# Asking for each stream transfer two steps after its piece instead of three

## The reference, cut to what matters

```python
xz = jnp.einsum('bld,ed->ble', hidden_states, in_proj_w)
x, z = jnp.split(xz, 2, axis=-1)
xc = silu(causal_conv(x))                        # 4 taps
x_dbl = jnp.einsum('bld,ed->ble', xc, x_proj_w)  # -> dt_r, Bc, Cc
delta = softplus(dt_r @ dt_proj_w.T + dt_proj_bias)
def step(h, inp):                                # over time, per channel and state n (16 of them)
    dA = jnp.exp(delta_t[..., None] * A)
    h = h * dA + (delta_t * x_t)[..., None] * B_t[:, None, :]
    y_t = jnp.einsum('bdn,bn->bd', h, C_t)
y = (y + xc * D_param) * silu(z)
x = x + y @ out_proj_w.T
x = x + moe(x @ W.T + adapter(x))                # 16 experts, top 4, and a shared expert
```

## Time and profile before

| | |
|---|---|
| median of 3 runs | 1827.28 us (1825.8 to 1832.31) |
| the profiled execution | 1825.8 us, its span 1824.0 us |
| mean granted TensorE clock | 0.961 of full speed |
| PE busy | 1656.9 us (91%) |
| DVE busy | 1418.4 us (78%) |
| POOL busy | 1090.5 us (60%) |
| ACT busy | 843.1 us (46%) |
| transfers of B rows (`b_all`) | 128, 256 KB each, 3.2 us from issue to landing (median) |
| transfers of weight tiles (`wt`) | 116, 256 KB each, 3.1 to 3.9 us (medians by source) |

### The profile page before, as it was taken

One profiled execution on the slowest core, in us unless ns is written; L12 is line 12 of the kernel. 1 busy time (PEld: TensorE's weight loads), 2 busy tenths in 40 slices (PEclk: granted clock), 3 DMA queues, 4 the chain that ended last, 5 costly groups with the idle time before them and its releaser, 6 DMA issues. The chain is left out here.

```text
span 1824.0 us, 28764 instructions
## 1 busy us (share of the span) xinstructions
PE 1656.9 (91%) x8052; PEld 1217.0 (67%) x8052; DVE 1418.4 (78%) x1889; ACT 843.1 (46%) x1276; POOL 1090.5 (60%) x860
## 2 busy tenths in 40 slices
PE   8678877999998999989888999999999999999997
PEld 5255544665555655555455657788788999999997
DVE  3699999999999999999999726777355656565654
ACT  2666766667767676766664411000122323322331
POOL 0299689997799986999988470000144434343443
PEclk9878989999999999999999999999999999999999
DMA  5122212232232232222214352112157566566664
GB/s 131 36 64 64 72 45 69 65 92 82 81 110 76 87 93 79 95 92 66 87 59 127 104 167 68 70 69 96 42 127 183 132 175 158 142 134 171 138 170 71
DMA packets 130025, 181.96 MB, mean 100 GB/s; under 512 B 21443, under 2 KB 79555, under 8 KB 126788
## 3 DMA queue, kind: packets, MB, share of 16 engines
q1 hardware_dynamic: 109540, 131.85, 22.5%
q0 software_dynamic: 17888, 43.79, 12.4%
q10 hardware_dynamic: 2432, 4.33, 0.9%
HBM read 276.18 MB, written 37.36 MB: 172 GB/s over the span
## 5 line engine op out<-in xcount | busy, mean ns | idle before, releaser
L1244 POOL TENSOR_TENSOR arena_kept<-arena_kept,b_all 128x512 f32<-128x512 f32 x512 | 637.0, 1274 | 184.5 <-DVE arena_kept L1136 104.2
L1136 DVE TENSOR_TENSOR_SCAN arena_kept<-da,arena_kept 128x512 f32<-128x512 f32 x512 | 597.9, 1214 | 15.1 <-issue 8.7
L963 ACT ACTIVATE da<-arena_kept,a_neg 128x504 f32<-128x504 f32 x512 | 344.5, 685 | 183.1 <-DVE arena_kept L1136 175.8
L736 PE MATMUL hT<-ident_kept,arena_kept 128*128 128x128 f32 x2048 | 309.9, 296 | 122.4 <-DVE arena_kept L1136 61.5
L736 PEld LDWEIGHTS hT<-ident_kept,arena_kept 128*128 128x128 f32 x2048 | 252.6, 152 | 224.7 <-DVE arena_kept L1136 133.8
L1152 DVE SCALAR_TENSOR_TENSOR yacc<-hT,c_now,yacc 128x512 f32<-128x512 f32 x452 | 316.5, 744 | 7.7 <-PE hT L736 6.7
L2168 POOL DMA_INDIRECT out<-y,slots_kept x76 | 133.9, 1762 | 240.3 <-issue 177.9
L527 PE MATMUL bank<-hid,wt 128*128 128x512 f32 x512 | 237.7, 610 | 0.7 <-ACT hid L786 0.7
L527 PEld LDWEIGHTS bank<-hid,wt 128*128 128x128 f32 x512 | 97.0, 199 | 101.1 <-issue 100.2
L2038 ACT ACTIVATE gs<-egp 128x352 f32<-128x352 f32 x73 | 33.8, 463 | 237.4 <-PE eup L1348 236.8
L1800 POOL DMA_DIRECT2D slots_kept<-lists_kept x1 | 0.6, 567 | 211.9 <-DVE lists_kept L1752 211.9
(11 more groups left out here) (249 smaller groups left out, 3198.2 us busy)
## 6 DMA issues: line engine op xcount, KB each, us to landing
w_up_kept<-in_up_T SPq DMA_DIRECT2D x76, 1408.0 KB, 5.9
w_dn_kept<-in_dn_T SPq DMA_DIRECT2D x76, 768.0 KB, 7.2
b_all<-bt_scratch SPq DMA_DIRECT2D x128, 256.0 KB, 3.2
wt<-in_in_T SPq DMA_DIRECT2D x64, 256.0 KB, 3.2
wt<-in_out_T SPq DMA_DIRECT2D x32, 256.0 KB, 3.5
res<-in_x_pad SPq DMA_DIRECT2D x16, 256.0 KB, 4.2
x_scratch<-res SPq DMA_DIRECT2D x16, 256.0 KB, 2.1
wt<-in_w_T SPq DMA_DIRECT2D x16, 256.0 KB, 3.1
```

The source lines that it names most:

```text
L736: mm = nc.tensor.transpose(turned_in(j, m, t)[:, d * P:(d + 1) * P], h[:, m % RING, d, t * P:(t + 1) * P], ident[:])
L963: nc.scalar.activation(out[:, :, 1:], rows[:, :, 1:], ACT.Exp, scale=a_neg[:, d, n:n + 1]) \
L1136: nc.vector.tensor_tensor_scan(h[:, n % RING, i, :], da[i % RING][:], dbx[:, i, :], 0.0, ALU.mult, ALU.add).then_inc(scan_done, 1)
L1244: nc.gpsimd.tensor_tensor(dbx[:, i, :], u[:, d, :], b_all[:, m % RING, :], ALU.mult) \
```

## The change

The constant `LATER = 3` is gone, and 2 stands in its five places. A transfer that belongs to a piece of step `m` is now in SP's list behind the B row of step `m + 2`, where it was behind that of step `m + 3`. What each transfer waits for is the same, and so are the instructions of the other four engines. No transfer is added or taken away.

```diff
 SLOTS = 6
-LATER = 3
@@ tiles_due
-            at = of * STEPS + step_of(piece) + LATER
+            at = of * STEPS + step_of(piece) + 2
@@ SP's loop over the steps m of block j
                     for t in range(TB if j else 0):
-                        if m == step_of(f"xr{t}") + LATER:
+                        if m == step_of(f"xr{t}") + 2:
                             store_x1("body", j, t)
                     if j == NBLK - 1 and m == step_of(f"xr{TB - 1}") + 4:
                         load_res(NBLK)
-                    if j and m == step_of(f"w{KM - 1}") + LATER:
+                    if j and m == step_of(f"w{KM - 1}") + 2:
                         store_x2T("body", j)
                     for t in range(TB if j else 0):
-                        if m == step_of(f"row{t}") + LATER:
+                        if m == step_of(f"row{t}") + 2:
                             store_x2("body", j, t)
-            for m in range(STEPS, STEPS + LATER):
+            for m in (STEPS, STEPS + 1):
```

## The result

The changed kernel takes 1841.9 us (median of 9 runs, 1835.84 to 1847.78), the kernel before 1829.09 us in the same comparison: a ratio of 1.0078, with a 95% interval of 1.0057 to 1.0099. It is slower by 13 us by the medians and by 14 us by the ratio, and the interval lies clear of 1. The forecast was 1836 us, with "the same" a little ahead of "slower". The measured time lies 0.1 us under the upper end of the range, 1842; the likeliest case did not come, and the loss was 1.3 to 1.5 times the sum of 9.6 us.

What follows compares the result with a forecast made beforehand. DVE, 97% busy in block 1, was taken to set the pace. Late B rows at steps 5, 9 and 12 cost 3.2 us in each of blocks 1 to 3, 9.6 in all: forecast 1836 us, range 1828 to 1842.

Steps and rivals of the forecast that it cites:

- SP's waits for `out` banks stand in front of B rows: SP's 64.6 us in 12 waits for PE's line 612 stand ahead of B rows, which would be issued later.
- Rival D: SP's waits are not in front of the B rows, so the time is unchanged, 1827 us; chance 0.04.
- Step 5: Its B row goes behind the tile of 352.42, lands 3.6 us after issue, and POOL starts 3.8 us late.
- The B row of step 7 is hidden: Behind `out2`/`out3`, it lands by 370.3, while the late POOL wants it at 372.0: no added loss.
- The lead of 1.8 us at step 7: POOL's smallest lead over DVE in steps 5 to 8; of POOL's 3.8 us, DVE loses 2.0.
- Steps 9 and 12: B rows behind `out4`/`out5` and `out6`/`out7`: POOL 4.3 and 5.0 us late, DVE's loss growing to 2.9 and 3.2.
- PE shifts by what DVE lost: `out5` starts later by DVE's 2.0 us; without such shifts the loss is 7.2 us in all, not 9.6.
- Other tiles and stores cost nothing: Steps 15 to 31: B rows later but in time; bounds 0 to 2 us per block for tiles, 1 for stores.
- Rival B: B rows come later still, at step 27 behind the 1 MB store and elsewhere: 1839 to 1843 us; chance 0.15.
- Nothing gained from earlier tiles and stores: PE has no wait of note for `wt`, ACT only 5.2 us for stores: gain 0, bound 5.2 us.
- rival C: Faster by earlier stores: `row1`'s store leaves sooner, ACT's `row3` copy doesn't wait, DVE gains: 1822 us; chance 0.04.
- rival A: The leads swallow more, or PE does not shift: loss 2.4 us or less per block, 1826 to 1833; chance 0.22.

Runs made afterwards that it cites:

- `out0` alone: Kernel before, with only the tile of `out0` asked for two steps after its piece (three transfers): 1837.35 us, ratio 1.0043.
- the injected gap: Kernel before, SP's list unchanged; PE waits for the next step's third scan before step 4's last four transposes in blocks 1 to 3: 1840.92 us, ratio 1.0061.

## Why the prediction was right and wrong, step by step

- *SP's waits for `out` banks stand in front of B rows.* Right. The run with only these tiles has the whole loss, the run without them none. Rival D is out.
- *Step 5: POOL 3.8 us late.* Right: 4.2, 3.7 and 4.0 us in blocks 1, 2 and 3. The landing was taken as 3.6 us and was 4.4 us in block 1, where two B rows and two tiles leave within 1.5 us.
- *The B row of step 7 is hidden.* Right in block 2, wrong in blocks 1 and 3, where `out3` was late itself: POOL went from 4.1 to 5.2 us late in block 1.
- *The lead of 1.8 us at step 7, DVE 2.0 us late.* Right in block 2: 1.9 us after step 7. In blocks 1 and 3 it was 3.6 and 3.2.
- *Steps 9 and 12: POOL 4.3 and 5.0 us late, DVE 2.9 and 3.2.* Here the sum came out too small. In block 2 POOL was 4.8 and 5.7 late, DVE 3.4 and 3.9: the chain worked as written, with one sixth missing. In block 3 POOL reached 9.3 and DVE 7.7 us.
- *PE shifts by what DVE lost.* This is the step that failed. The sum let PE's pieces start later by DVE's delay and put any growth of PE's own time at nothing, without naming it. The rows were there: PE is back to back from step 3 to 7, and a granted clock of 0.97 says that it isn't always at the upper level. What the runs show in its place: a gap of 0.85 us was followed by 3.4 us at half clock in `out0` alone, and so was the injected gap (1.7, 1.7 and 3.4 us) in each block, where DVE lost about twice what the gap had gained in length. DVE's lateness at step 14 summed over the three blocks was 16.3, 17.6 and 13.2 us in the three traces of the changed kernel, 6.7, 8.0 and 3.6 us over the sum of 9.6, with 13.7, 17.1 and 10.3 us more at the lower clock than before. DVE's waits for PE's transposes grew by 7.4 us in the first trace, those for POOL by 6.1. Where the clock did nothing more than before (block 1 of the third trace), DVE was 3.5 us late and the sum's 3.2 was near.
- *Other tiles and stores cost nothing.* Right, with 21.9 us of late B rows that DVE doesn't feel. Rival B named step 27: POOL waits there in block 3, and nothing passes, so it is by coincidence that the measured time lies in that rival's range of 1839 to 1843. In blocks 1 and 2 luck had a part. "After that POOL's lead is larger" does not hold to the end of the block: in the kernel before the lead falls from 2.2 us at step 27 to 0.3 at step 30, and the row behind the 1 MB store came 1.0 and 0.9 us before POOL wanted it.
- *Nothing gained from earlier tiles and stores.* Right; rival C is out. The Trainium skill's rule ("DMA: Bandwidth & Descriptors", "Rules for kernel authors", issue early and wait late) did not help, as SP's wait came with it. The Trainium skill's fit in the same page ("Anatomy of one DMA") is for GpSimd's queue and gives 2.6 us as an estimate. These rows of SP's queue do not show it: 3.7 to 4.4 us for the four rows of block 1 that POOL waited for, each with another transfer close by.
- *The split of the chances.* The border of 0.5% lay in the middle of the forecast, and rival A, PE not shifting, got 0.22 for a smaller loss that the trace did not bear out; no rival had PE's time growing. With a term for it, the forecast would have lain over the border.

What stays open: why the clock fell behind some gaps and not behind others. In the three traces of the changed kernel, gaps of PE of 1.1, 1.2 and 0.7 us stood at step 4 of block 1, and the clock fell behind the first alone. How much of the loss is PE's therefore changes from execution to execution, and no run takes it out of the changed kernel: the one that filled a gap got nothing back. In block 3 there are also stretches of low clock behind step 6 that no experiment ties to a gap.

## What to carry to other kernels

A queue that serves two consumers should have, ahead of each urgent transfer, only waits that are already over when it is reached; here the tiles' waits ended just when POOL released the B row, and one step nearer put the urgent one behind them. To price a late transfer, take its lateness, subtract the smallest lead downstream until the late engine next idles, and then ask of the engine that gets the rest whether it is back to back itself. Where TensorE is, as here, an added gap of 1.7 us cost about twice its length, and one of 0.5 us its own length where the clock stayed high. Take also the least lead of the whole stretch, not only of the steps next to the change. And before a profile is used to explain a median, compare its own time with that median: four of the profiles here lay 3.3 to 11 us over theirs.

## What the runs showed of the hardware that was not expected

- A gap of PE can be enough for 3.4 us at the lower level of the clock (0.52 and 0.57 granted), which begin in the gap or within 1.2 us behind it. At step 4 of blocks 1 and 2, where PE is otherwise back to back, this followed gaps of 0.76, 0.85, 1.06 and 1.68 us (twice), and did not follow eight gaps of 0.37 to 0.65 us or one of 1.21. At the same step of block 3, where the kernel before has a gap of 1.72 us and no fall, it followed the seven gaps of 2.28 to 3.42 us and none of the seven of 1.7 us or the one of 1.92. Eight products took 4.51 to 4.85 us with the clock low and 3.60 otherwise.
- Where the clock is low can repeat closely: the three profiles of the kernel before have it at the same places of blocks 1 to 3, within 0.2 us measured from the block's first scan, but for two stretches in the last steps of block 2 that differ by 3.4 us. It need not: the three profiles of the changed kernel differ, in that the clock fell at step 4 of block 1 in one of them and at step 4 of block 3 in two.
- A B row of 256 KB lands 3.0 to 3.8 us after its issue (median 3.1) when no other transfer is issued within 4 us. With another one issued within 1 us the median over the 15 traces is 3.7; in steps 5 to 13 of block 1 it is 3.6 to 4.1 in the kernel before and 3.7 to 4.8 in the changed one. Behind the 1 MB store it is 5.1 to 5.8 us in 12 cases.
